# Three accumulators instead of four, eight gathers and then eight scatters a round, and a reordered first round in a one-core graph layer

## The chip, the cores and the metric

The kernel runs on one core of one Trainium2 chip. The metric is the device time of one execution in microseconds (us); lower is better. Three runs of the kernel before are at hand, and one further execution was profiled.

## The reference, cut to what matters

The program is one layer of a graph network over 6250 nodes with 256 features and 100000 edges, followed by a recurrent network over the nodes. The part that the change touches is the sum over the edges:

```python
xn = layernorm(x)
neigh = segment_sum(xn[src], dst, num_segments=n)   # 100000 rows gathered, summed by target
h = (1 + eps) * xn + neigh
h = relu(h @ W1 + b1) @ W2 + b2                      # then a batch norm over the nodes
x = x + h + attention_mix(xn)                        # linear attention: keys, values, queries
x = x + lstm_stage(layernorm(x))                     # 6250 sequential steps
```

## The kernel before, in words

The program is a row of blocks, and each block begins when all engines have ended the one before.

**Opening** (lines 174 to 266). `x` is loaded and normalised, and `xn_d`, the normalised rows in device memory, is stored. Between these stores SP issues the zeros for the accumulators `acc_d`, ten pieces of 640 KB for each of NA = 4 accumulators: 8 pieces first, 2 after each of ten pairs of stores, and the 12 that are left at the end (line 194).

**First edge block** (helpers from line 328, engine programs from line 513 to 708). The edges are taken in groups of 512, four columns of 128. A round is two groups, g = 0 and g = 1, and there are H2 = 50 rounds in this block. For each group:

- SP loads the source and target indices into `staged_i` (line 339), when the gathers of the same g a round earlier have landed and both its targets have been cast.
- POOL gathers four times 128 rows of `xn_d` into `rows` (line 348). `gather_group(h, g)` first waits for the sum of the group (h-1, g), since that sum reads the same half of `rows`.
- PE transposes the targets (line 378), and DVE compares them, which gives the 0/1 matrix `equal` (line 426), finds the rows that must go to a spare row because an earlier edge of the group has the same target (lines 429 to 434), and writes `target` (line 439). That last write waits until the scatters of (h-1, g) have landed, since they read the same half of `target`.
- PE multiplies `equal` with `rows` (line 389), which adds up edges with the same target; ACT copies the product to `sums` (line 400), also only after the scatters of (h-1, g) have landed. `sum_equal` waits for the copy of the group before, since there is one set of banks.
- POOL scatters the four columns with an accumulating indirect DMA (line 367). Column j goes to accumulator j, and a scatter waits until the last one into its accumulator has landed.

POOL's order in a round i of the first block is: gathers of (i, 1), scatters of (i, 0), gathers of (i+1, 0), scatters of (i, 1). In the same round the other engines also make keys and values for 125 nodes. On DVE (lines 671 to 703) the order is: casts; `find_equal(i, 0)`; keys and values, centred; `find_equal(i, 1)` with its `target` write; the variance, the root and `kvn` (lines 689 to 698); then `kvsum`. On PE (lines 583 to 604) it is: targets of (i, 0); the product for keys and values; targets of (i, 1); `sum_equal(i, 0)`; the product of `kvn` (line 597), which waits for DVE's `kvn`; `sum_equal(i, 1)`; the transposes of the next node rows. So `sum_equal(i, 1)` stands behind `kvn` of the same round, and `kvn` behind the `target` write of (i, 1). ACT (lines 627 to 639) squares, copies sums (i, 0), takes the root, copies sums (i, 1), and copies the next node rows. In rounds 1 to 9 some weights for the later stage are turned and split as well.

**Second edge block** (lines 741 to 866). Rounds 50 to 97, with the same groups; beside two rounds runs one chunk of 250 nodes of the attention: four products on PE. No key or value work stands between the two sums of a round.

**The stage after the edges** (lines 893 to 1060). For each of 25 chunks, SP loads the chunk's rows of all accumulators into `ht` (line 918), DVE adds them in two steps (lines 928 and 930) into `hsum`, PE transposes `hsum` (line 988), and two layers of products follow. **The rest** is a normalisation and the recurrent network, which no line of the change touches.

Of the kernel before, what the change touches and what calls it, by code (L numbers as in the profile page):

```python
# [27 lines left out]
ALU = mybir.AluOpType  # L28
# [13 lines left out]
GT = 4  # L42
# [5 lines left out]
NA = 4  # L48
# [10 lines left out]
ZS = 10  # L59
# [35 lines left out]
def gps_layer_kernel(nc, x, src, dst, gnn_eps, gW1, gb1, gW2, gb2, gamma, beta, w_qkv, b_qkv,  # L95
# [14 lines left out]
    with top, stage, nc.allow_non_contiguous_dma(reason="vectors of 256 numbers, loaded once"):  # L110
# [157 lines left out]
        with ExitStack() as st:  # L268
# [41 lines left out]
            scattered = [[sem(f"scattered{a}_{g}") for g in range(2)] for a in range(NA)]  # L310
# [42 lines left out]
            def scatter_group(pool, h, g, of=FULL):  # L353
# [4 lines left out]
                for j in range(T):  # L358
                    a = j
                    if not due(h) and not g:  # L360
                        pool.wait_ge(zero_out[a], 16 * (ZS + (a == NA - 1)))
                    if g:
                        pool.wait_ge(scattered[a][0], 16 * (h + 1))
                    elif due(16 * h):
                        pool.wait_ge(scattered[a][1], 16 * h)
# [4 lines left out]
                    ).then_inc(scattered[a][g], 16)  # L370
# [22 lines left out]
            def copy_sums(act, h, g, of=FULL):  # L393
                P, T = of
                act.wait_ge(summed, 2 * h + g + 1)
                for a in range(NA):
                    if due(16 * h):
                        act.wait_ge(scattered[a][g], 16 * h)
# [13 lines left out]
            def find_equal(dve, h, g, of=FULL):  # L412
# [23 lines left out]
                for a in range(NA):  # L436
                    if due(16 * h):
                        dve.wait_ge(scattered[a][g], 16 * h)
# [117 lines left out]
            def _(pool):  # L556
# [18 lines left out]
            def _(pe):  # L575
                kv_to = bank[3][0:R, :].rearrange("p (s h c) -> p s h c", s=2, h=HEADS)

                def body(i):
                    turn_targets(pe, i, 0)
                    if not due(i):  # L580
                        pe.wait_ge(mixw_in, 16 * MIX_LOADS)
# [9 lines left out]
                    sum_equal(pe, i, 0)  # L591
# [14 lines left out]
                turn_rows(pe, 0)  # L606
# [3 lines left out]
            def _(act):  # L610
# [16 lines left out]
                def body(i):  # L627
                    act.wait_ge(cen_ready, i + 1)
                    nc.scalar.activation(sq[:], cen[:], ACT.Square).then_inc(sq_ready, 1)
                    copy_sums(act, i, 0)  # L630
# [10 lines left out]
                copy_rows(act, 0)  # L641
# [3 lines left out]
            def _(dve):  # L645
# [7 lines left out]
                add_rows(dve, 0)  # L653

                def body(i):
# [18 lines left out]
                    if not due(i):  # L674
                        dve.wait_ge(mixw_in, 16 * MIX_LOADS)
# [1055 lines left out]
```

## Time and profile before

| | us |
|---|---|
| three runs | 16084.22, 16095.17, 16082.19; median 16084.22 |
| profiled execution, its own time | 16096.5 |
| its span | 16094.8 |
| PE busy | 12549.7 (78%) |
| DVE busy | 10109.2 (63%) |
| ACT busy | 5158.2 (32%) |
| POOL busy | 2040.0 (13%), all of it before 2664 |
| both edge blocks with the gaps between | 120 to 2671 |

POOL is GpSimd, DVE VectorE, ACT ScalarE, PE TensorE, SP SyncE. The shares over the whole span say little here: the recurrent network takes 13064 us of the 16095 and hides the stages before it. The edge blocks have to be read by themselves, in their own windows and in the timeline of a round.

### The profile page before, as it was taken

The page shows a single profiled execution, that of the slowest core. Times are in us where ns is not written, and L with a number is a line of the kernel's source. Part 1 is how long each engine was busy: PE and PEld are TensorE (multiplying, and loading weights), DVE is VectorE, ACT ScalarE, POOL GpSimd, SP SyncE. Part 2 cuts the span into 40 slices and gives each one's busy share as a digit, 9 for nine tenths or more (in the row PEclk, how much of TensorE's full clock was granted, in tenths as well). Part 3 has the DMA queues.
Part 4 walks back from the last instruction along what each step waited for, and adds up shares of the span by engine and source line. Part 5 has one row for each costly group of instructions (what it writes and reads, how often), then busy time and mean ns, then how long its engine had stood idle before and what let it go on. Part 6 is the DMA issues. An engine that isn't in the chain of part 4 may idle for free. (4 is left out here: it accounts for less than half of the span.)

```text
span 16094.8 us, 920575 instructions
## 1 busy us (share of the span) xinstructions
PE 12549.7 (78%) x375284; PEld 11596.3 (72%) x375284; DVE 10109.2 (63%) x84155; ACT 5158.2 (32%) x32368; POOL 2040.0 (13%) x1573
## 2 busy tenths in 40 slices
PE   3444446888888888888888888888888888888887
PEld 2333334788888888888888888888888888888886
DVE  4443222666666666666666666666666666666667
ACT  1111111333333333333333333333333333333333
POOL 5887885000000000000000000000000000000000
PEclk8666777555555555555555555555555555555556
DMA  6555554100000000000000000000000000000000
GB/s 169 90 91 84 83 83 99 67 2 2 2 2 2 2 2 2 2 2 2 2 2 2 2 2 2 2 2 2 2 2 2 2 2 2 2 2 2 2 2 17
DMA packets 622798, 340.12 MB, mean 21 GB/s; under 512 B 455829, under 2 KB 571433, under 8 KB 622134
## 3 DMA queue, kind: packets, MB, share of 16 engines
q0 software_dynamic: 150048, 204.90, 7.9%
q1 hardware_dynamic: 461968, 129.69, 3.9%
q10 hardware_dynamic: 10742, 5.06, 0.1%
q8 instruction: 19, 0.31, 0.0%
q14 instruction: 21, 0.16, 0.0%
HBM read 172.29 MB, written 160.65 MB: 21 GB/s over the span
## 5 line engine op out<-in xcount | busy, mean ns | idle before, releaser
L1363 PE MATMUL bank<-hrest,whh 128*128 128x1 bf16 (+1 forms) x300000 | 9080.9, 166 | 1920.2 <-DVE hrest L1487 1920.2
L1363 PEld LDWEIGHTS bank<-hrest,whh 128*128 128x128 bf16 x300000 | 8555.7, 104 | 2483.1 <-DVE hrest L1487 2482.7
L1431 ACT ACTIVATE gates<-bank 128x4 f32<-128x4 f32 x12500 | 2198.1, 176 | 8137.1 <-DVE bank L1468 7260.1
L1468 DVE TENSOR_REDUCE bank<-bank 128x4 f32<-128x12 f32 x12500 | 2212.9, 177 | 3178.9 <-PE bank L1363 2296.2
L1363 PE MATMUL bank<-xsteps,wih 128*128 128x15 bf16 (+1 forms) x60048 | 2715.4, 174 | 0.0
L1476 DVE CUSTOM_DVE_ANT_1 uv<-gates 128x4 f32<-128x4 f32 x12500 | 2041.6, 163 | 445.9
L1363 PEld LDWEIGHTS bank<-xsteps,wih 128*128 128x128 bf16 x60048 | 2278.7, 103 | 0.0
L1439 ACT ACTIVATE bank<-gates 128x1 f32<-128x1 f32 x12500 | 2188.1, 175 | 119.3
L1492 DVE TENSOR_TENSOR hrest<-hrest 128x1 f32<-128x1 f32 x12500 | 1993.3, 159 | 216.2
L1497 DVE TENSOR_TENSOR hrest<-hrest 128x1 f32<-128x1 f32 x12500 | 1981.5, 159 | 217.3
L1363 PE MATMUL bank<-ones,gbias 128*128 128x5 bf16 x10008 | 1679.9, 168 | 9.7 <-DMA xsteps<-x_d 9.7
L367 POOL DMA_INDIRECT acc_d<-sums,target x782 | 1263.5, 1616 | 255.9 <-issue 237.2
L389 PE MATMUL bank<-rows,equal 128*128 128x256 f32 x1564 | 688.4, 617 | 771.9 <-DMA rows<-xn_d,staged_i 729.9
L1435 ACT ACTIVATE og<-zo 128x1 f32<-128x1 f32 x6250 | 1171.4, 187 | 0.0
L389 PEld LDWEIGHTS bank<-rows,equal 128*128 128x128 f32 x1564 | 479.1, 321 | 918.7 <-issue 815.4
L1363 PEld LDWEIGHTS bank<-ones,gbias 128*128 128x128 bf16 x10008 | 1039.6, 104 | 10.1 <-issue 10.1
L1476 DVE DVE_READ_ACCUMULATOR2_ANT gates<- 128x1 f32 x12500 | 1040.1, 83 | 0.0
L1472 DVE TENSOR_REDUCE zo<-bank 128x1 f32<-128x3 f32 x6250 | 980.2, 157 | 0.0
L1487 DVE SCALAR_TENSOR_TENSOR hrest<-gates,bank 128x1 f32<-128x1 f32 x6250 | 970.8, 155 | 11.7
L1487 DVE SCALAR_TENSOR_TENSOR hrest<-og,bank 128x1 f32<-128x1 f32 x6250 | 972.1, 156 | 0.0
L348 POOL DMA_INDIRECT rows<-xn_d,staged_i x782 | 775.3, 991 | 248.2 <-issue 225.0
L400 ACT ACTIVATE sums<-bank 128x512 f32<-128x512 f32 x391 | 212.3, 595 | 1507.0 <-PE bank L389 1500.8
(167 smaller groups left out, 3295.4 us busy)
## 6 DMA issues: line engine op xcount, KB each, us to landing
acc_d<-zero SPq DMA_DIRECT2D x40, 640.0 KB, 12.6
ht<-acc_d SPq DMA_DIRECT2D x100, 224.0 KB
xsteps<-x_d SPq DMA_DIRECT2D x1252, 15.0 KB, 1.7
U<-hrest SPq DMA_DIRECT2D x1250, 5.0 KB, 1.7
x_d<-x SPq DMA_DIRECT2D x25, 750.0 KB, 3.2
rows<-xn_d,staged_i POOLq DMA_INDIRECT x782
acc_d<-sums,target POOLq DMA_INDIRECT x782, 3.8
xi<-xn_d SPq DMA_DIRECT2D x50, 125.0 KB
```

The lines of the kernel that those rows point to most:

```text
L367: pool.indirect_dma_start(out=acc_d[a], out_offset=bass.IndirectOffsetOnAxis(ap=target[0:P, g, j:j + 1], axis=0), in_=sums[0:P, g, j, :], ...
L389: last = nc.tensor.matmul(prod[j // 2][0:P, j % 2, :], equal[0:P, g, j, 0:P], rows[0:P, g, j, :], start=True, stop=True)
L1363: return nc.tensor.matmul(to, w, v, start=start, stop=True, skip_group_check=True)
L1431: nc.scalar.activation(gates[:, k, 0:2 * NG_[k]:2], zi[k], ACT.Tanh).then_inc(ifg_act[k], 1)
L1435: nc.scalar.activation(og[1], zo[:], ACT.Tanh).then_inc(o_act, 1)
L1439: nc.scalar.activation(tc[k], gates[:, k, 5:6], ACT.Tanh).then_inc(tc_ready[k], 1)
L1468: nc.vector.tensor_reduce(zi[k], gi[k][b][:, s], axis=AX.X, op=ALU.add).then_inc(ifg_summed[k], 1)
L1472: nc.vector.tensor_reduce(zo[:], go[b][:, s], axis=AX.X, op=ALU.add).then_inc(o_summed, 1)
L1476: nc.vector.tensor_tensor_reduce(out=uv[:, k, :].rearrange("p (a c) -> p a c", a=2), in0=gates[:, k, 0:4].rearrange("p (a c) -> p a c", a= ...
L1487: stt(out=hrest[:, 0, at, k:k + 1], in0=og[k], scalar=1.0, in1=tc[k], op0=ALU.add, op1=ALU.mult).then_inc(h1_ready[k], 1)
L1492: nc.vector.tensor_tensor(hrest[:, 1, at, k:k + 1], hrest[:, 0, at, k:k + 1], hpart[:, 0, at, k:k + 1], ALU.subtract).then_inc(h2_ready[k], 1)
L1497: nc.vector.tensor_tensor(hrest[:, 2, at, k:k + 1], hrest[:, 1, at, k:k + 1], hpart[:, 1, at, k:k + 1], ALU.subtract).then_inc(h3_ready[k], 1)
```

## The change

It does five things. The number of accumulators falls from four to three, with their zeros and loads. A round's eight scatters go to accumulators 0, 1, 2, 0, 1, 2, 0, 1, each waiting for the one three places before it, or, for the first three, for the last one of the round before into the same accumulator. POOL's order becomes both gather groups of round i+1, then both scatter groups of round i. In round 0 the targets, the sum and the copy of group (0, 0) go ahead of the node rows, keys and values. The sum over accumulators in the later stage becomes two additions of one accumulator each.

```diff
-NA = 4
+NA = 3
 def scatter_group(pool, h, g, of=FULL):
                 for j in range(T):
-                    a = j
-                    if not due(h) and not g:
-                        pool.wait_ge(zero_out[a], 16 * (ZS + (a == NA - 1)))
-                    if g:
-                        pool.wait_ge(scattered[a][0], 16 * (h + 1))
-                    elif due(16 * h):
-                        pool.wait_ge(scattered[a][1], 16 * h)
+                    place = GT * g + j
+                    a = place % NA
+                    if place >= NA:
+                        before = place - NA
+                        pool.wait_ge(scattered[before % GT][before // GT], 16 * (h + 1))
+                    else:
+                        if not due(h):
+                            pool.wait_ge(zero_out[a], 16 * (ZS + (a == NA - 1)))
+                        before = 2 * GT - 1
+                        while before % NA != a:
+                            before -= 1
+                        if due(16 * h):
+                            pool.wait_ge(scattered[before % GT][before // GT], 16 * h)
...
 # POOL, first edge block
                 gather_group(pool, 0, 0, first=True)
+                gather_group(pool, 0, 1, first=True)
                 def body(i):
-                    gather_group(pool, i, 1)
+                    gather_group(pool, i + 1, 0)
+                    gather_group(pool, i + 1, 1)
                     scatter_group(pool, i, 0)
-                    gather_group(pool, i + 1, 0)
                     scatter_group(pool, i, 1)
                 first_apart(pool, H2 - 1, body)
-                gather_group(pool, H2 - 1, 1)
                 scatter_group(pool, H2 - 1, 0)
                 scatter_group(pool, H2 - 1, 1)
...
 # PE, first edge block
                     turn_targets(pe, i, 0)
                     if not due(i):
+                        sum_equal(pe, i, 0)
+                        turn_rows(pe, i)
                         pe.wait_ge(mixw_in, 16 * MIX_LOADS)
...
                     turn_targets(pe, i, 1)
-                    sum_equal(pe, i, 0)
+                    if due(i):
+                        sum_equal(pe, i, 0)
...
 # POOL, second edge block
                 gather_group(pool, H2, 0)
-                with pool.Fori(H2, HL, 1) as h:
-                    gather_group(pool, h, 1)
+                gather_group(pool, H2, 1)
+                with pool.Fori(H2, HL - 1, 1) as h:
+                    gather_group(pool, h + 1, 0)
+                    gather_group(pool, h + 1, 1)
                     scatter_group(pool, h, 0)
-                    gather_group(pool, h + 1, 0)
                     scatter_group(pool, h, 1)
+                gather_group(pool, HL, 0)
                 gather_group(pool, HL, 1, of=LAST)
+                scatter_group(pool, HL - 1, 0)
+                scatter_group(pool, HL - 1, 1)
...
 # DVE, the stage after the edges
-                    nc.vector.tensor_tensor(ht[:, b, 0:2], ht[:, b, 0:2], ht[:, b, 2:4], ALU.add).then_inc(pair_ready, 1)
+                    nc.vector.tensor_tensor(ht[:, b, 0], ht[:, b, 0], ht[:, b, 1], ALU.add).then_inc(pair_ready, 1)
                     dve.wait_ge(pair_ready, c + 1)
-                    nc.vector.tensor_tensor(hsum[:, b], ht[:, b, 0], ht[:, b, 1], ALU.add).then_inc(hsum_ready, 1)
+                    nc.vector.tensor_tensor(hsum[:, b], ht[:, b, 0], ht[:, b, 2], ALU.add).then_inc(hsum_ready, 1)
```

On ACT and DVE of the first block round 0 is reordered in the same way (`copy_sums(0, 0)` and `copy_rows(0)` first; `add_rows(0)` behind `find_equal(0, 0)`). No line of DVE, PE or ACT changes for the rounds from 1 on, apart from the names of the semaphores that they wait for.

## Rows read from the trace of the kernel before

**Rows 1.** Page, section 2: the span in 40 slices, busy tenths of each.

```profile
POOL 5887885000000000000000000000000000000000
PEclk8666777555555555555555555555555555555556
```

**Rows 2.** Windows by stage: length, then busy time and (count) per engine, PEclk, DMA share, GB/s.

```profile
165.56:1417.32 1251.76, 556.99 (x1760) 392.96 (x1760) 611.93 (x1385) 188.00 (x449) 1017.41 (x768) 0.68 0.55 91
...
1461.00:2650.06 1189.06, 581.12 (x1785) 448.04 (x1784) 283.48 (x633) 142.48 (x283) 961.31 (x748) 0.71 0.52 83
...
2671.45:2897.00 225.55, 187.65 (x900) 160.55 (x900) 88.78 (x137) 63.77 (x152) 0.00 (x0) 0.96 0.39 118
...
3030.00:16094.00 13064.00, 11069.89 (x370356) 10483.85 (x370356) 8957.28 (x81487) 4704.76 (x31352) 0.00 (x0) 0.50 0.02 2
```

**Rows 3.** Groups on POOL, window 165.56:1417.32: busy us, mean ns, idle before and releasers.

```profile
L367 POOL DMA_INDIRECT acc_d<-sums,target x384 | 634.3, 1652 | 117.3 <-issue 116.7 <-ACT sums L400 0.6
L348 POOL DMA_INDIRECT rows<-xn_d,staged_i x384 | 383.2, 998 | 117.0 <-issue 103.9 <-ACT sums L400 10.1 <-DMA acc_d<-sums,target 2.7
```

**Rows 4.** The same for the window 1461:2650.06.

```profile
L367 POOL DMA_INDIRECT acc_d<-sums,target x376 | 594.5, 1581 | 117.1 <-issue 113.7 <-ACT sums L400 2.7 <-PE bank L389 0.3
L348 POOL DMA_INDIRECT rows<-xn_d,staged_i x372 | 366.8, 986 | 113.4 <-issue 113.4
```

**Rows 5.** Timeline of one round: start, us, engine, line, operation, idle time before it.

```profile
999.99 1.02 POOL L348 DMA_INDIRECT rows<-xn_d,staged_i  x1 [0.30 <-issue]
...
1002.05 0.16 DVE L439 TENSOR_TENSOR target<-dstf,move 128x4 int32<-128x4 f32 x1 [7.29 <-DMA acc_d<-sums,target]
...
1002.61 0.94 POOL L348 DMA_INDIRECT rows<-xn_d,staged_i  x1 [0.30 <-issue]
...
1005.11 2.13 POOL L367 DMA_INDIRECT acc_d<-sums,target  x1 [0.30 <-issue]
...
1006.50 0.69 DVE L698 TENSOR_TENSOR kvn<-kvn,kv_b 125x512 f32<-125x512 f32 x1
...
1007.25 1.22 PE L597 MATMUL bank<-kvn 125*128 125x128 f32 x4 [9.72 <-DVE kvn L698]
...
1008.26 3.13 PE L389 MATMUL bank<-rows,equal 128*128 128x256 f32 x8
...
1011.30 1.55 POOL L367 DMA_INDIRECT acc_d<-sums,target  x1 [0.30 <-issue]
...
1018.71 1.62 POOL L367 DMA_INDIRECT acc_d<-sums,target  x1 [0.30 <-issue]
```

**Rows 6.** Timeline, the last rounds of the first edge block.

```profile
1415.75 1.57 POOL L367 DMA_INDIRECT acc_d<-sums,target  x1 [0.31 <-issue]
...
1425.57 3.62 PE L389 MATMUL bank<-rows,equal 128*128 128x256 f32 x8
...
1429.23 1.08 ACT L400 ACTIVATE sums<-bank 128x512 f32<-128x512 f32 x2 [8.06 <-PE bank L389]
1431.19 1.55 POOL L367 DMA_INDIRECT acc_d<-sums,target  x1 [1.03 <-issue]
```

**Rows 7.** Tile acc_d, window 165.56:1417.32.

```profile
DMA to landing us min/median/max: 3.6/3.8/4.4
```

**Rows 8.** Timeline of the opening: the last zero stores, and the start of the first edge block.

```profile
99.01 19.24 SPq L194 DMA_DIRECT2D acc_d<-zero  x14
...
136.17 0.38 ACT L527 ACTIVATE xk<-bank 128x250 f32<-128x250 f32 x1 [87.59 <-PE bank L519]
...
151.32 3.23 PE L389 MATMUL bank<-rows,equal 128*128 128x256 f32 x8
...
163.99 1.57 POOL L367 DMA_INDIRECT acc_d<-sums,target  x1 [0.31 <-issue]
```

**Rows 9.** Waits of PE in the stage after the edges: us, times, longest.

```profile
PE bank L988 <- DVE hsum L930: 15.6, 20, 1.8
```

**Rows 10.** Groups on DVE in the same stage.

```profile
L928 DVE TENSOR_TENSOR ht<-ht 125x1024 f32<-125x1024 f32 x25 | 30.6, 1224 | 26.1 <-DMA ht<-acc_d 25.4
```

More of the change, by code:

```diff
@@ L309, in gps_layer_kernel @@
             gathered = [sem(f"gathered{g}") for g in range(2)]
-            scattered = [[sem(f"scattered{a}_{g}") for g in range(2)] for a in range(NA)]
+            scattered = [[sem(f"scattered{j}_{g}") for g in range(2)] for j in range(GT)]
             cast, dst_turned = sem("cast"), sem("dst_turned")
@@ L369, in scatter_group @@
                         in_=sums[0:P, g, j, :], in_offset=None, compute_op=ALU.add,
-                    ).then_inc(scattered[a][g], 16)
+                    ).then_inc(scattered[j][g], 16)
             def turn_targets(pe, h, g, of=FULL):
@@ L395, in copy_sums @@
                 act.wait_ge(summed, 2 * h + g + 1)
-                for a in range(NA):
+                for j in range(GT):
                     if due(16 * h):
-                        act.wait_ge(scattered[a][g], 16 * h)
+                        act.wait_ge(scattered[j][g], 16 * h)
                 for m in range(T // 2):
@@ L435, in find_equal @@
                                                     in1=dup[0:P, 0:T], op0=ALU.subtract, op1=ALU.mult))
-                for a in range(NA):
+                for j in range(GT):
                     if due(16 * h):
-                        dve.wait_ge(scattered[a][g], 16 * h)
+                        dve.wait_ge(scattered[j][g], 16 * h)
                 nc.vector.tensor_tensor(target[0:P, g, 0:T], dstf[0:P, g, 0:T], move[0:P, 0:T], ALU.subtract)\
@@ L627, in body @@
                 def body(i):
+                    if not due(i):
+                        copy_sums(act, i, 0)
+                        copy_rows(act, i)
                     act.wait_ge(cen_ready, i + 1)
                     nc.scalar.activation(sq[:], cen[:], ACT.Square).then_inc(sq_ready, 1)
-                    copy_sums(act, i, 0)
+                    if due(i):
+                        copy_sums(act, i, 0)
                     act.wait_ge(gvar_ready, i + 1)
@@ L652, in _ @@
                 links = 5 + REFINE_STEPS
-                add_rows(dve, 0)
                 def body(i):
@@ L674, in body @@
                     if not due(i):
+                        add_rows(dve, i)
                         dve.wait_ge(mixw_in, 16 * MIX_LOADS)
@@ L752, in _ @@
                 gather_group(pool, H2, 0)
-                with pool.Fori(H2, HL, 1) as h:
-                    gather_group(pool, h, 1)
+                gather_group(pool, H2, 1)
+                with pool.Fori(H2, HL - 1, 1) as h:
+                    gather_group(pool, h + 1, 0)
+                    gather_group(pool, h + 1, 1)
                     scatter_group(pool, h, 0)
-                    gather_group(pool, h + 1, 0)
                     scatter_group(pool, h, 1)
+                gather_group(pool, HL, 0)
                 gather_group(pool, HL, 1, of=LAST)
+                scatter_group(pool, HL - 1, 0)
+                scatter_group(pool, HL - 1, 1)
                 scatter_group(pool, HL, 0)
                 scatter_group(pool, HL, 1, LAST)
-                for a in range(NA):
-                    pool.wait_ge(scattered[a][0], 16 * (HL + 1))
-                    pool.wait_ge(scattered[a][1], 16 * (HL + (a < LAST[1])))
+                for j in range(GT):
+                    pool.wait_ge(scattered[j][0], 16 * (HL + 1))
+                    pool.wait_ge(scattered[j][1], 16 * (HL + (j < LAST[1])))
             @block.tensor
```

2 lines of the change are left out of this document (removed).

## The prediction

> **What bounds the kernel now.** Times of the trace are in us. I read the slices of the page first [rows 1]: POOL works only at the start, and what the change touches lies there. The windows by stage [rows 2] then put a length on it: 1251.8 for 48 rounds of the first edge block, 1189.1 for most of the second, 225.6 for the stage after the edges, 13064 for the recurrent network, which the change leaves alone. In both edge blocks POOL is the busiest engine (81%); DVE has 49% and 24%, and the DMA engines are busy 0.55 and 0.52.
>
> Whether POOL is really the limit shows in its groups [rows 3, 4]: 384 gathers of 0.998 and 384 scatters of 1.652 in the first block, 0.986 and 1.581 in the second, and before each of them an idle time of 0.305 put down to "issue", nothing else to speak of. Eight of each with their gaps are 8 x (1.303 + 1.957) = 26.1 a round, and the window gives 1251.76 / 48 = 26.08. So POOL never stands still in the first block; a round costs what its sixteen DMA instructions cost. The same for the second: 8 x (1.291 + 1.886) = 25.4.
>
> The change neither adds nor removes one of these sixteen. It can gain only in what lies around them, and lose wherever POOL begins to wait. So the next view is the timeline of a round [rows 5], to see how much room each of POOL's waits has.
>
> **The wait that the new order meets.** Call the end of the last scatter of (i-1, 1) the mark. In the round shown it is at 999.69 (999.99 less the gap of 0.30). Behind it a chain runs over four engines: the scatter lands, DVE's `target` write of (i, 1), which waited 7.29 for that landing, begins at 1002.05; the variance, root and `kvn` end at 1007.19; PE's product of `kvn` begins at 1007.25, and `sum_equal(i, 1)` runs from 1008.26 to 1011.39. That is 11.7 after the mark. At the end of the block [rows 6] the mark is 1417.32 and the same sum ends at 1429.19: 11.9. Over all rounds of the window I take 12.0.
>
> Who needs this sum? The gathers of (i+1, 1), which overwrite the half of `rows` that it reads. Before the change they come a whole round after the mark, 26 against 12, and POOL meets the wait long satisfied. After it POOL's order behind the mark is gathers (i+1, 0), then gathers (i+1, 1): only four gathers, 4 x 1.303 = 5.2, lie between. The chain itself is not shortened, because no line of DVE or PE changes for rounds from 1 on: `sum_equal(i, 1)` still stands behind `kvn`, and `kvn` behind the landing of scatters that are now directly ahead of the gathers. So POOL must stop there in every round, and behind the stopped gathers are queued the eight scatters that start the next chain. The cycle closes on itself.
>
> Its length: 12.0 to the end of the sum; then POOL's waking. A gather's waking from a stop is not shown for this semaphore; the nearest row is a scatter that waited for ACT's copy: the copy ended at 1430.31, the scatter began at 1431.19 [rows 6], so 0.9. The bounds are 0.1 (the releases between the other engines in rows 5) and 1.0. Then four gathers with three gaps, 4 x 0.998 + 3 x 0.305 = 4.9, and eight scatters with eight gaps, 8 x 1.957 = 15.7. Together 33.5.
>
> Two small things come off. A first gather behind scatters takes 1.02 against 0.94 for a later one, a first scatter 1.62 against 1.55 [rows 5]; with the second of each run that is some 0.1 for each change of kind, and there are half as many: 0.1 off the scatters. And the scatters average 1.652 here against 1.581 in the second block; the excess, 8 x 0.071 = 0.57 a round, sits in single scatters such as the one at 1005.11, which took 2.13 while DVE made `kvn` [rows 3, 4, 5]. In the new order `kvn` falls into POOL's gathers and its stop, but other DVE work falls on the scatters. I take half off, 0.3. The Trainium skill ("SBUF — State Buffer", section "Who interferes with whom") has a rule for this: a VectorE instruction with two SBUF inputs contends with a GpSimd instruction that reads SBUF. By it the `kvn` multiplication and addition would no longer lengthen scatters, and the whole 0.57 could go, 13 us more off the sum than my half; the trace agrees as far as the one long scatter shows.
>
> A round of the first block becomes 33.5 - 0.1 - 0.3 = 33.0 (rounded down), 6.9 more than 26.1, and from the last scatter of round 0 to that of round 48 there are 48 such rounds: **+331**.
>
> I looked for a second stop in this block. Scatters (i, 0) now land 7.6 before those of (i, 1), and DVE needs about 5 from the `target` write of (i, 0) to the next one; the gathers of (i+1, 0) need `sum_equal(i, 0)`, which stands ahead of `kvn`; the indices are loaded a round earlier than before. Each has more than 2 to spare.
>
> **The opening.** Ten of forty pieces of zeros go. The last fourteen took SP 19.24 to issue [rows 8], 1.37 each, so the block could begin 13.7 earlier; the last stores of `xn_d`, issued just before these fourteen, must land first, and I take 12. Round 0: ACT's own DMA issues stand before its first copy at 136.17, so reordering round 0 moves the keys and values no further forward than those 12. `sum_equal(0, 1)` ended at 154.55 [rows 8], now 142.5; but the gathers of (1, 1) wait for it and the scatters of round 0 for them: 142.5 + 0.9 + 4.9 + 15.7 = 164.0 for the end of the last scatter of round 0, against 165.56 before. **-2.** The 12 gained are nearly all eaten by the new order at once; bounds -12 and +5.
>
> **The end of the first block.** The last copy waits for the same chain and `sum_equal(49, 1)` before and after: nothing, within 2.
>
> **The second block.** No `kvn` stands between the sums. `sum_equal(h, 1)` needs the copy of (h, 0), which needs the landing of scatters (h-1, 0). From their end: 2.3 to the landing (3.8 from a scatter's start, less its 1.57 [rows 7, 6]), 1.1 for a copy, 3.1 to 3.6 for the sum and about 2 for an attention product between, 0.9 to wake: 10. Between them and the gathers of (h+1, 1) lie four scatters and four gathers, 12.7. The wait is covered with 2 or 3 to spare; if that cover is gone, each us costs 47. What is left is one change of kind fewer per round, 2 x 0.1: **-9**. Its start and its end I put at **-2** together (the start has a sum to wait for before the second gathers; at the end gathers come earlier), within 5.
>
> **Three accumulators.** A scatter now waits for the third before it. That one lands 3.6 to 4.4 after its start [rows 7] and the scatter starts 3 x 1.86 = 5.6 after it; with 0.9 to wake, 5.3 at most. Nothing, by 0.3.
>
> **The stage after the edges.** PE waited 15.6 over 20 chunks for `hsum` [rows 9]. The first addition, 1.224 on 1024 elements [rows 10], becomes one of half the size, some 0.69, and a quarter less is loaded. That takes 0.53 x 20 = 11 off, up to 15.6: **-13**. The recurrent network: nothing.
>
> **The sum.** 331 - 2 - 9 - 2 - 13 = **+305**. Against the profiled execution's own 16096.5 (its span is 16094.8) that is 16401.5; this execution stands 12.3 above the median of the three runs, 16084.2, so for a median I forecast 16084.2 + 305, about **16390**, 1.9% slower.
>
> **Rivals.**
> 1. *The chain is faster than I take it.* PE's part, 1.0 to the sum and 3.1 to 3.6 for it, is at a granted clock of half (1.2 GHz) much of the time; the windows' mean is 0.68 [rows 2]. At 2.4 GHz about 2 of the 12 would go, and with a wake of 0.1 a little more: some 100 to 130 off, about 16280. For it speaks that the mean is not 0.5; against it that PE will be idle longer in each round, with the same work.
> 2. *No stop: faster.* If `sum_equal(i, 1)` ended within 5.2 of the mark, POOL would stay the limit and only the gains would be left: 12 from the opening, 0.2 x 97 = 19 from fewer changes of kind, 13 from the later stage, 44 in all: 16040. The deciding point is the place of the gathers of (i+1, 1), 5.2 behind the mark; the rows show 11.7 and 11.9, and landing plus DVE alone are 7.5. For it speaks only that DVE or PE might have slack that I read as need.
> 3. *Scatters queue behind one another.* If in a run of eight the landing came at 4.9 or later instead of 3.8, each wait on three accumulators would bite; at 0.9 more per three scatters, 0.3 x 760 = 228 on top: 16620. Against it: the DMA engines are busy 0.55, and no landing of the window is over 4.4.
> 4. *The cover in the second block is thinner than 2*: 47 per us, inside the range above the forecast.
>
> **Chances.** Forecast with the upper part of rival 4: 0.74. Rival 1: 0.13. Rival 2: 0.06, with 0.02 for a change within the bound. Rival 3: 0.05. A measurement of this kernel can tell about 0.2%, 32 us, from no change; so faster 0.06, same 0.02, slower 0.92. Bounds of a round's excess are 5.2 (most of rival 1 with a short waking) and 7.6 (nothing taken off): 250 to 365, less 26 and 10 either way: 16290 to 16450.
>
> **What would show it.** In the first edge block POOL idle about 7 to 8 in each round in front of the gathers of (i+1, 1), released by PE's sum (or ACT's copy after it), a period near 33, and POOL's share down from 81% to about 64%; the second block with POOL's gaps at 0.305 throughout and a period near 25.2; `hsum` waits gone on PE. A first block with rounds near 26 makes the forecast wrong and rival 2 right; gaps in front of single scatters inside a run speak for rival 3.

## The result, and the profile after

Four runs of each kernel on one chip: 16373.65 after the change (median; 16369.55 to 16377.94) against 16084.92 before (16082.19 to 16095.17). The ratio is **1.0179**, 95% interval 1.0166 to 1.0192: slower, 288.7 us by the medians. The forecast was 16390.

The profiled executions are 16096.5 before and 16369.55 after, 273.0 apart. The one of before lies above all four of its runs, that of after is the lowest of its four; that makes the rest of the 288.7. Cut at marks that both traces have, the 273.0 fall on these pieces:

| piece | before | after | difference | predicted |
|---|---|---|---|---|
| start to the end of round 0's last scatter | 165.56 | 160.85 | -4.7 | -2 |
| 48 rounds of the first edge block | 1251.76 | 1572.18 | +320.4 | +331 |
| from there to the last scatter of all | 1246.25 | 1238.04 | -8.2 | -11 |
| from there to the recurrent network's first load (3030.52 and 3314.29) | 366.95 | 343.22 | -23.7 | -13 |
| the rest | 13064.3 | 13053.5 | -10.8 | 0 |
| sum | | | +273.0 | +305 |

The windows by stage of the kernel after (length, busy time and count per engine, PEclk, DMA share, GB/s): first block, second block with the boundary before it, the stage after the edges (all 25 chunks), the recurrent network.

```profile
160.85:1733.03 1572.18, 492.47 (x1760) 360.23 (x1760) 607.26 (x1385) 182.97 (x448) 983.63 (x769) 0.64 0.44 73
1733.03:2971.07 1238.04, 582.15 (x1854) 447.62 (x1855) 288.04 (x666) 147.67 (x295) 985.42 (x772) 0.67 0.52 82
2978.90:3195.60 216.70, 193.76 (x938) 170.10 (x938) 82.03 (x158) 70.81 (x167) 0.00 (x0) 0.93 0.32 94
3314.29:16367.80 13053.51, 11066.50 (x370356) 10480.01 (x370356) 8937.23 (x81487) 4680.37 (x31352) 0.00 (x0) 0.50 0.02 2
```

In the first line POOL has the same 768 instructions as in [rows 2] (and one at the window's edge), and even 34 less busy time, in a window 320 longer: its share fell from 81% to 63%. The page's slices say the same at a glance. Where [rows 1] had 8, 8 and 7 in the second to fourth slice, there is now 6, 6 and 6, and POOL works one slice longer:

```profile
POOL 4666788200000000000000000000000000000000
PEclk7666666755555555555555555555555555555556
```

POOL's groups in the first edge block, window 160.85:1733.03 (busy us, mean ns, idle before and releasers):

```profile
L373 POOL DMA_INDIRECT acc_d<-sums,target x385 | 611.6, 1589 | 118.1 <-issue 110.9 <-DMA acc_d<-sums,target 7.2
L348 POOL DMA_INDIRECT rows<-xn_d,staged_i x384 | 373.7, 973 | 470.7 <-issue 470.7
```

Its waits in the same window (us in total, times, longest):

```profile
POOL rows L348 <- issue: 470.7, 384, 7.9
POOL acc_d L373 <- issue: 110.9, 362, 0.5
POOL acc_d L373 <- DMA acc_d<-sums,target: 7.2, 23, 0.5
```

Against [rows 3] one number has changed much: the idle time ahead of the gathers, 117.0 to 470.7. That is 354 more, over 48 rounds 7.4 a round; the longest single stop is 7.9. The instructions themselves have become a little shorter: a scatter fell from 1.652 to 1.589, a gather from 0.998 to 0.973, 0.7 a round together. What is left is 320.4 / 48 = 6.67 more a round, a period of 32.75.

Where the stop stands in a round shows in the timeline (start, us, engine, line, operation, idle time before it):

```profile
1011.07 1.74 POOL L373 DMA_INDIRECT acc_d<-sums,target  x1 [0.30 <-issue]
...
1015.22 0.16 DVE L445 TENSOR_TENSOR target<-dstf,move 128x4 int32<-128x4 f32 x1 [2.86 <-DMA acc_d<-sums,target]
...
1016.97 0.95 POOL L348 DMA_INDIRECT rows<-xn_d,staged_i  x1 [0.30 <-issue]
...
1019.62 0.69 DVE L709 TENSOR_TENSOR kvn<-kvn,kv_b 125x512 f32<-125x512 f32 x1
...
1020.36 1.23 PE L606 MATMUL bank<-kvn 125*128 125x128 f32 x4 [22.61 <-DVE kvn L709]
...
1021.38 3.35 PE L395 MATMUL bank<-rows,equal 128*128 128x256 f32 x8
...
1025.53 0.94 POOL L348 DMA_INDIRECT rows<-xn_d,staged_i  x1 [7.61 <-issue]
...
1030.68 1.63 POOL L373 DMA_INDIRECT acc_d<-sums,target  x1 [0.30 <-issue]
```

The last scatter of the round before ends at 1012.81: that is the mark. From it the landing and `target` take 2.4, `kvn` is ready at 7.5, the sum begins at 8.6 and ends at 11.9, and the gather that needs its half of `rows` starts 0.80 later. POOL had ended the four gathers before it at 1017.92 and stood for 7.61. PE's product waited 22.61 for `kvn`: no other work of PE lies between. The landing is as before in the median [rows 7]; the longest is 4.8 where it was 4.4. `acc_d` in this window:

```profile
DMA to landing us min/median/max: 3.6/3.8/4.8
```

In the second edge block the period is 25.27 against 25.42 and POOL's gaps stay at 0.31 in the mean (window 1775:2936.34; the periods of this block are taken over the 44 rounds that end with its 46th):

```profile
L373 POOL DMA_INDIRECT acc_d<-sums,target x368 | 577.1, 1568 | 112.8 <-issue 105.5 <-DMA acc_d<-sums,target 7.3
L348 POOL DMA_INDIRECT rows<-xn_d,staged_i x368 | 360.1, 979 | 112.6 <-issue 101.0 <-DVE target L445 5.8 <-ACT sums L406 5.8
```

Beside [rows 4], the scatters went from 1.581 to 1.568. The opening's timeline shows the ten pieces of zeros gone (4 issued at the end instead of the 14 of [rows 8]) and two stops of POOL in their place, one for the indices of group (1, 0) and one for the sum of (0, 1):

```profile
100.91 5.33 SPq L194 DMA_DIRECT2D acc_d<-zero  x4
...
129.55 0.95 POOL L348 DMA_INDIRECT rows<-xn_d,staged_i  x1 [10.65 <-DMA staged_i<-in_dst]
...
140.56 0.95 POOL L348 DMA_INDIRECT rows<-xn_d,staged_i  x1 [6.11 <-issue]
```

In the stage after the edges PE no longer waits for `hsum` at all ([rows 9]: 15.6), and the whole stage took 216.70 against 240.00 before (2671.45 to 2911.45; the window of [rows 2] stops at 2897, before the last chunks are done).

### The profile page after: what moved, and what is told of

Its sections match the earlier page's. It is cut to its first block and busy times, and to the rows that moved or that the text cites. A ratio compares the mean times of both kernels' runs of the same rounds, so it can differ in the third digit from the quotient of the medians.

```text
span 16367.8 us, 920271 instructions
## 1 busy us (share of the span) xinstructions
PE 12450.8 (76%) x375284; PEld 11540.8 (71%) x375284; DVE 10061.5 (61%) x84155; ACT 5128.3 (31%) x32368; POOL 1999.1 (12%) x1573
## 5 line engine op out<-in xcount | busy, mean ns | idle before, releaser
L395 PE MATMUL bank<-rows,equal 128*128 128x256 f32 x1564 | 544.8, 510 | 437.0 <-ACT sums L406 426.3
L606 PE MATMUL bank<-kvn 125*128 125x128 f32 x200 | 61.1, 461 | 1054.9 <-DVE kvn L709 1054.9
```

## The experiments

The theory (A): POOL's new order closes a cycle over landing, `kvn`, PE's sum and the gathers, and costs the 330; the three accumulators cost nothing and gain a little. The main rival (B): the three accumulators or the longer waits of scatters are what costs. Kernels are called by the number of their experiment, so kernel 2 is that of experiment 2. Gaps and periods below are read from each kernel's timeline as in the table above. Where a kernel was timed several times (kernels 1, 2, 8 and 10), its median and its ratio to the kernel before stand, with a 95% interval; the others have a single time, given beside the median of the kernel before on the same chip.

### 1. The order undone, three accumulators kept

```diff
                 def body(i):
-                    gather_group(pool, i + 1, 0)
-                    gather_group(pool, i + 1, 1)
+                    gather_group(pool, i, 1)
                     scatter_group(pool, i, 0)
+                    gather_group(pool, i + 1, 0)
                     scatter_group(pool, i, 1)
```

(with `gather_group(pool, H2 - 1, 1)` behind the loop again; first block only)

> The changed kernel with one part undone: in the first edge block POOL takes gathers (i, 1), scatters (i, 0), gathers (i+1, 0), scatters (i, 1) again; three accumulators, the new first round, the new order of the second block and the additions stay. Theory A (the gathers of (i+1, 1) stand too close behind the scatters of (i-1, 1), and the sum they wait for ends 12 us after them): the stop of 7.1 us a round goes, a round of the first block is 26.1 us, and the kernel takes about 16373.7 less 320 = 16050 us. Rival B (three accumulators make the scatters wait): the loss stays, 16370 us, with idle time in front of scatters.

Measured: 16047.15, ratio 0.9973 (0.9963 to 0.9984). Period 26.11, round 0 ends at 149.11. POOL's groups of the first block, window 149.11:1402.53:

```profile
L373 POOL DMA_INDIRECT acc_d<-sums,target x384 | 635.0, 1654 | 119.0 <-issue 106.6 <-PE bank L395 6.7 <-DMA acc_d<-sums,target 3.7
L348 POOL DMA_INDIRECT rows<-xn_d,staged_i x384 | 382.4, 996 | 117.0 <-issue 103.3 <-ACT sums L406 10.1 <-DMA acc_d<-sums,target 3.3
```

The idle time ahead of the gathers, 470.7 in the kernel after, is 117.0 again, with three accumulators. B falls. One edit of POOL's order is worth 1.0179 against 0.9973, about 330 us: 48 x (32.75 - 26.11) = 319 in the rounds and 160.85 - 149.11 = 12 in round 0.

### 2. The new order kept, PE's sum ahead of `kvn`

```diff
+                    sum_equal(pe, i, 1)
                     pe.wait_ge(kvn_ready, i + 1)
...
                     last.then_inc(kv_prod, 1)
-                    sum_equal(pe, i, 1)
```

> The changed kernel with POOL's order kept and the chain cut instead: on PE sum_equal(i, 1) stands directly behind sum_equal(i, 0), ahead of the product of kvn. Theory A: the sum then needs only the targets' comparison and ACT's copy of (i, 0), both done before the last scatter of the round before, so POOL has no stop; a round of the first block is 25.3 us, as in the second block, and the kernel takes 16373.7 less 48 x 7.4 = 355, about 16020 us, less than both kernels. Rival B: nothing changes, 16370 us. Rival C (POOL stops for the landing of eight scatters in a row, whatever PE does): rounds stay near 32 us.

Measured: 16047.61, ratio 0.9974 (0.9963 to 0.9984). The stops are gone from all rounds of the block but the first, which shows that the cycle closed through PE's program order and not through the data. But the period is 26.11, not 25.3. POOL's groups, window 159.09:1412.47:

```profile
L373 POOL DMA_INDIRECT acc_d<-sums,target x384 | 615.4, 1603 | 119.9 <-issue 109.4 <-DMA acc_d<-sums,target 10.5
L348 POOL DMA_INDIRECT rows<-xn_d,staged_i x384 | 401.0, 1044 | 117.0 <-issue 103.6 <-ACT sums L406 13.4
```

No gap has grown; but beside kernel 1 the gathers have grown, from 0.996 to 1.044, while the scatters fell only from 1.654 to 1.603. The reason shows in a round of this kernel's timeline:

```profile
1002.74 0.69 DVE L707 TENSOR_TENSOR kvn<-cen,grstd 125x512 f32<-125x512 f32 x1
1002.80 1.45 POOL L348 DMA_INDIRECT rows<-xn_d,staged_i  x1 [0.30 <-ACT sums L406]
...
1004.19 0.69 DVE L709 TENSOR_TENSOR kvn<-kvn,kv_b 125x512 f32<-125x512 f32 x1
1004.55 1.14 POOL L348 DMA_INDIRECT rows<-xn_d,staged_i  x1 [0.30 <-issue]
...
1006.00 0.95 POOL L348 DMA_INDIRECT rows<-xn_d,staged_i  x1 [0.30 <-issue]
...
1019.69 0.69 DVE L695 TENSOR_TENSOR cen<-kv,gsum 125x512 f32<-125x512 f32 x1
1019.75 2.06 POOL L373 DMA_INDIRECT acc_d<-sums,target  x1 [0.30 <-issue]
```

A gather that starts 0.06 into a DVE multiplication with both inputs in SBUF takes 1.45, one with none beside it 0.95; the scatter that starts 0.06 into `cen` takes 2.06 instead of 1.55. How far into the instruction it starts matters: the gather that starts 0.36 into `kvn`'s addition takes only 1.14. The new order moves the `kvn` instructions from the scatters onto the gathers and takes little off. And in round 0 POOL stood 13.75 for the indices of (1, 0), since this kernel too gathers round 1 before it scatters round 0:

```profile
133.22 0.98 POOL L348 DMA_INDIRECT rows<-xn_d,staged_i  x1 [13.75 <-DMA staged_i<-in_dst]
```

So eight and eight without the stop is worth no more than the old order.

### 3. The new order with four accumulators

```diff
-NA = 3
+NA = 4
```

(with the two additions of the kernel before)

> The changed kernel with four accumulators again (zeros, scatters to accumulators 0 to 3 twice, four loads and the addition of 1024 elements in the later stage), POOL's new orders kept. Theory A: the first block keeps its rounds of 32.75 us and its stops of 7.1 us; only the opening (12 us later), and the stage after the edges (23 us longer) go back, about 16405 us. Rival B: the stops go and the kernel is near 16090 us.

Measured: 16424.12 (before 16091.63). Period 32.71, and 48 stops of 6.82 to 7.88, mean 7.62. POOL's gathers in the window 178.67:1748.92, and the stage after the edges with PE's waits in it:

```profile
L348 POOL DMA_INDIRECT rows<-xn_d,staged_i x384 | 375.1, 977 | 468.3 <-issue 468.3
```

```profile
2993.90:3234.99 241.09, 199.23 (x938) 169.10 (x938) 96.46 (x158) 70.69 (x167) 0.00 (x0) 0.93 0.37 111
```

```profile
PE bank L1003 <- DVE hsum L945: 16.7, 21, 1.8
```

The stop is the same with four accumulators. Against the kernel after, 17.8 are lost by the end of round 0 (178.67 against 160.85) and 24.4 in the stage after the edges (241.09 against 216.70). Both are larger than the prediction had taken (12 for the zeros, 13 for the stage). The next two take the 24 apart.

### 4. A fourth load in the stage after the edges

```diff
-                    for a in range(NA):
-                        rows_ = acc_d[a][...]
+                    for a in range(NA + 1):
+                        rows_ = acc_d[a % NA][...]
```

(the kernel after, with room for the fourth part and its wait; the additions leave the fourth part out)

> The changed kernel with a fourth, unused load in the stage after the edges (accumulator 0 once more, into a fourth part of ht, and waited for); the additions stay two of 512 elements. The stage took 240.0 us before and 216.7 us after. If the smaller addition gave the 23 us, the stage stays at 217 us. If the loads did (PE waited for sums that waited for loads), it goes back to 235 to 240 us. Everything ahead of the stage stays as it is.

Measured: 16391.07 (before 16091.63). The stage and PE's waits in it:

```profile
2984.55:3213.61 229.06, 198.05 (x938) 171.47 (x938) 83.13 (x158) 70.70 (x167) 0.00 (x0) 0.92 0.39 117
```

```profile
PE bank L1003 <- DVE hsum L945: 7.0, 9, 1.1
```

That is 12.4 over the 216.70, between the two expectations: the fourth load alone costs half of the difference.

### 5. The wide addition, with three loads

```diff
-nc.vector.tensor_tensor(ht[:, b, 0], ht[:, b, 0], ht[:, b, 1], ALU.add)
+nc.vector.tensor_tensor(wide[:, b], ht[:, b, 0:2], ht[:, b, 1:3], ALU.add)
```

(on kernel 1, `hsum` then from `wide[:, b, 0]` and `ht[:, b, 2]`: two columns of 512 added, as before the change)

> x1_order_undone with a first addition of 1024 elements in the stage after the edges (half of it unused, into a tile of its own), three loads as they are. x4_fourth_load gave 229.1 us for the stage against 216.7 in the changed kernel and 240.0 before: a quarter more loading costs 12. If the rest is the addition, the stage is here 216.7 + 11 to 13, about 229 us; if PE has slack for 0.5 us a chunk once the loads are early, it stays at 217 to 219 us, and loads and addition cost only together.

Measured: 16053.96 (before 16087.83). The stage in kernel 1, then in this one with PE's waits:

```profile
2650.44:2867.75 217.31, 193.71 (x938) 170.14 (x938) 82.12 (x158) 70.70 (x167) 0.00 (x0) 0.93 0.32 94
```

```profile
2659.95:2886.45 226.50, 199.73 (x938) 170.16 (x938) 95.82 (x158) 70.68 (x167) 0.00 (x0) 0.92 0.30 90
```

```profile
PE bank L1004 <- DVE hsum L946: 3.7, 15, 0.4
```

That is 9.2 more. With the 12.4 of the load it makes 21.6 of the 23.3 by which the stage fell.

### 6. Two accumulators

```diff
-NA = 3
+NA = 2
```

(on kernel 2, with one addition in the later stage)

> x2_sum_ahead with two accumulators (two loads and one addition in the later stage). A scatter then waits for the second before it, which starts 3.7 us earlier and lands 3.8 us after its start. If POOL's waking of 0.8 to 0.9 us comes on top of every such wait, a scatter inside a run starts 4.7 us after the second before it: 0.5 us more for each of six scatters of a run, 2.9 us a round, 98 rounds, 285 us; less some 30 to 35 for fewer zeros, loads and additions: about 16300 us. If only the landing counts (POOL's sequencer waits ahead of the engine), it costs 0.1 us a wait at most: 16020 to 16070 us, and three accumulators have 1.8 us of room instead of 0.9.

Measured: 16331.15 (before 16087.83). Periods 29.21 and 28.22, against 26.11 and 25.23 in kernel 2: 3.1 and 3.0 more a round. POOL's scatters, window 150.16:1552.23, and three in a row from the second block's timeline:

```profile
L373 POOL DMA_INDIRECT acc_d<-sums,target x384 | 623.4, 1624 | 261.9 <-DMA acc_d<-sums,target 155.3 <-issue 106.5
```

```profile
2000.93 1.55 POOL L373 DMA_INDIRECT acc_d<-sums,target  x1 [1.17 <-DMA acc_d<-sums,target]
2002.85 1.56 POOL L373 DMA_INDIRECT acc_d<-sums,target  x1 [0.37 <-issue]
2005.46 1.55 POOL L373 DMA_INDIRECT acc_d<-sums,target  x1 [1.05 <-DMA acc_d<-sums,target]
```

Two scatters start 1.92 and 2.61 apart in turn, 4.53 from one to the next into the same accumulator. That is about the landing, 3.8 after the start in the median, and 0.79 for POOL to wake: where this trace shows a scatter waiting for a landing, it starts 0.79 after it nearly every time. With three accumulators the starts are 5.6 apart: about 1 to spare. The stage after the edges stays at 216.7, so going from three accumulators to two brings nothing there; with three, PE already never waited for `hsum`.

### 7. Kernel 2 without two of `kvn`'s instructions

```diff
-step(nc.vector.tensor_tensor(kvn[:], cen[:], spread(grstd[:]), ALU.mult))
-step(nc.vector.tensor_tensor(kvn_s, kvn_s, gain_of(kv_g), ALU.mult))
-nc.vector.tensor_tensor(kvn_s, kvn_s, gain_of(kv_b), ALU.add).then_inc(kvn_ready, 1)
+nc.vector.tensor_tensor(kvn[:], cen[:], spread(grstd[:]), ALU.mult).then_inc(kvn_ready, 1)
```

This leaves out gain and bias of the normalised keys and values.

> x2_sum_ahead without the gain and the bias of the normalised keys and values (DVE's multiplication and addition, 0.69 us each with both inputs in SBUF, left out; one chain link fewer for each). In x2_sum_ahead a round of the first block takes 26.1 us although POOL has no stop, against 25.2 in the second block: gathers average 1.044 us against 0.974. Theory A: DVE instructions with both inputs in SBUF lengthen POOL's indirect DMAs that run beside them; without these two, gathers go back to about 0.98 and a round to about 25.6 us, 20 to 25 us less in all. Rival: the longer gathers have to do with the traffic of the scatters that land at that time, or with the order of gathers and scatters; then the round stays at 26.1 us.

Measured: 16043.81 (before 16087.83). Period 25.78, 0.33 less. The gathers average 1.015 instead of 1.044. In the timeline one long gather is left, beside the one instruction that is left:

```profile
1016.02 0.69 DVE L707 TENSOR_TENSOR kvn<-cen,grstd 125x512 f32<-125x512 f32 x1
1016.09 1.44 POOL L348 DMA_INDIRECT rows<-xn_d,staged_i  x1 [0.30 <-ACT sums L406]
1017.83 0.95 POOL L348 DMA_INDIRECT rows<-xn_d,staged_i  x1 [0.30 <-issue]
```

In kernel 2 the gather after the long one took 1.14; here it takes 0.95. The direction is as expected, the size is not (0.33 against 0.5). The trace of kernel 2 shows why: in nearly every round one gather starts 0.06 into `kvn`'s first multiplication (0.48 a round), and one 0.36 into its addition (0.20 a round). Leaving out the last two instructions takes away only the second. Of 48 x 0.33 = 16, 5.9 are left at the last scatter of all, since this kernel's second block ran at 25.46 a round, 0.23 above kernel 2's, with no edit there.

### 8. Kernel 2 with round 0's first scatters ahead

```diff
                 def body(i):
+                    if not due(i):
+                        scatter_group(pool, i, 0)
                     gather_group(pool, i + 1, 0)
                     gather_group(pool, i + 1, 1)
-                    scatter_group(pool, i, 0)
+                    if due(i):
+                        scatter_group(pool, i, 0)
                     scatter_group(pool, i, 1)
```

> The changed kernel with sum_equal(i, 1) ahead of the product of kvn (as in x2_sum_ahead), and in round 0 alone POOL scatters (0, 0) before it gathers round 1. In x2_sum_ahead POOL stood 13.8 us in the opening in front of the gathers of (1, 0), for their indices, with the sums of (0, 0) ready; in x1_order_undone the first scatter started at 123.4 and round 0 ended at 149.1, against 159.1. If that idle time is worth filling, round 0 ends about 10 us earlier than in x2_sum_ahead and the whole is near 16037 us; if POOL is held by sum (0, 1) or its copy anyway, nothing changes, 16047 us.

Measured: 16042.35, ratio 0.9972 (0.9962 to 0.9983). Round 0 ends at 150.32 instead of 159.09, 8.8 earlier: POOL scatters in the time in which it stood for indices. At the last scatter of all 2.1 of that is left (2642.33 against 2644.45); the second block's period was 25.34 against 25.23, again with no edit there. The totals of kernels 2 and 8 are not told apart.

### 9. The old first round

Kernel 1 with `turn_rows(0)`, `copy_rows(0)` and `add_rows(0)` ahead of the loops, and the sum and the copy of (0, 0) where they were before.

> x1_order_undone with the first round of the kernel before on PE, ACT and DVE as well (node rows, keys and values of round 0 ahead of its targets and sums). In x1_order_undone the first scatter started at 123.4 us (128.9 in x7_wide_add, whose opening is the same) and the last of round 0 ended at 149.1 (155.3). If the reordered first round is worth something, the first scatter waits here for ACT's copy behind the centred keys and values, about 12 us earlier than the 145.5 of the kernel before: near 133, and round 0 ends at 153 to 156. The rival is that the second group's copy sets the end of round 0 in any case, so that it ends at 149 to 152.

Measured: 16043.86 (before 16106.83 on that chip). The first scatter starts at 132.2, against 123.4 in kernel 1 and 128.9 in kernel 5, which has the same opening as kernel 1. Round 0 ends at 152.81, against 149.11 and 155.28. Two kernels with the same opening differ by 6 at the end of round 0, and the old first round lies between them there, though its first scatter is the latest of the three by 3: what the reordering of round 0 is worth could not be told.

### 10. Kernel 8 with `earlier` made from PSUM

```diff
+for j in range(T):
+    made = nc.vector.scalar_tensor_tensor(out=earlier[0:P, j, 0:P], in0=turned[0:P, j, 0:P],
+                                          scalar=dstf[0:P, g, j:j + 1], in1=below[0:P, 0:P],
+                                          op0=ALU.is_equal, op1=ALU.mult)
 nc.vector.tensor_tensor(equal[0:P, g, 0:T, 0:P], turned[0:P, 0:T, 0:P], mine, ALU.is_equal)
-step(nc.vector.tensor_tensor(earlier[...], equal[...], below[...], ALU.mult))
```

`turned` is a PSUM bank, so the 512-element instruction with two inputs from SBUF is replaced by four of 128 with one.

> x6_first_scatters with DVE's product for earlier duplicates (equal by below, 128x512, both inputs in SBUF) replaced by four instructions that compare the targets in PSUM with the column's own target and multiply by below in one step (one tensor input in SBUF). If instructions with two SBUF inputs lengthen POOL's indirect DMAs, the long gathers and scatters beside them go in both blocks: a round of the first block falls from 26.13 to about 25.9 us and of the second from 25.34 to 25.2, 10 to 20 us in all, near 16027 us. If not, the time stays at 16042 us; if the comparison that now comes about 1 us later delays a sum on which POOL waits, it rises.

Measured: 16045.71 against 16106.83 on that chip, ratio **0.9962** (0.9948 to 0.9975), the lowest of all; kernel 8 has 0.9972, and the intervals overlap. Periods 25.90 and 25.12, against 26.14 and 25.34 in kernel 8; the last scatter of all ends at 2623.86, 18.5 earlier than in kernel 8. The total doesn't show it: in the profiled execution the recurrent network, which no edit touches, took 25.4 more than in kernel 8's. The groups of the first block, 150.74:1394.18:

```profile
L373 POOL DMA_INDIRECT acc_d<-sums,target x385 | 610.5, 1586 | 120.6 <-issue 106.3 <-DMA acc_d<-sums,target 13.7 <-PE bank L395 0.3
L348 POOL DMA_INDIRECT rows<-xn_d,staged_i x384 | 397.2, 1034 | 117.0 <-issue 107.6 <-ACT sums L406 9.4
```

And two scatters of a round, beside the DVE instructions that start near them:

```profile
1004.26 1.55 POOL L373 DMA_INDIRECT acc_d<-sums,target  x1 [0.30 <-DMA acc_d<-sums,target]
1004.32 0.69 DVE L700 TENSOR_TENSOR cen<-kv,gsum 125x512 f32<-125x512 f32 x1
...
1006.08 0.69 DVE L437 TENSOR_TENSOR equal<-bank,dstf 128x512 f32<-128x512 f32 x1
1006.12 1.57 POOL L373 DMA_INDIRECT acc_d<-sums,target  x1 [0.30 <-issue]
```

A scatter that starts 0.04 into a DVE instruction with one input in PSUM takes 1.57, as if nothing were beside it. One that started 0.06 ahead of `cen` was not lengthened either, where kernel 2's, 0.06 behind its start, took 2.06. So a kernel's time also depends on the phase, that is, on how often a start happens to fall into such an instruction.

How much is phase can be counted in the traces. The table takes the same 44 rounds of the second block in six kernels whose code for these rounds is the same, but for kernel 10's edit. It has the gathers and scatters that start while `earlier` is being made, and what they take over the ordinary 0.95 and 1.55 (0.07 more for the first of a run):

| kernel | starts inside `earlier` | extra, a round | period | period less extra |
|---|---|---|---|---|
| after | 32 | 0.15 | 25.27 | 25.12 |
| 1 | 28 | 0.19 | 25.29 | 25.11 |
| 2 | 28 | 0.12 | 25.23 | 25.11 |
| 7 | 44 | 0.34 | 25.46 | 25.12 |
| 8 | 34 | 0.23 | 25.34 | 25.11 |
| 10 | 37, and none lengthened | 0.00 | 25.12 | 25.12 |

This one instruction accounts for the differences between the second blocks. The kernels with the old instruction differ by phase; kernel 10's 0.22 a round against kernel 8 is the instruction that went. In the first block it is less clear: of the 0.24 that kernel 10 gained there, 0.09 stood beside `earlier` in kernel 8, and most of the rest beside `cen` and `kvn`, which are unchanged: phase.

## Why the prediction was right

**The stop.** Its place (ahead of the gathers of (i+1, 1)), its size and its cause came as written: stops of 7.1 to 7.9, mean 7.7, where 7 to 8 stood, a period of 32.75 where 33.0 stood, POOL at 63% where 64% stood. (The range of 16290 to 16450 is rounded outward: the sums given for it make 16298 and 16433.) The chain's terms, as means over the 48 rounds: the sum ended 11.99 behind the mark (taken 12.0), POOL woke 0.80 after it, in every one of them (taken 0.9, between bounds of 0.1 and 1.0), four gathers took 4.80 (taken 4.9), and eight scatters with their gaps 15.16 (taken 15.7, less the 0.4 that comes off). Together they are the 32.75. That the cause is the place of PE's sum behind `kvn` is shown by kernel 2. Kernel 1 shows that without POOL's new order in the first block the rest of the change costs nothing. Rival 1, a faster chain, did not come: the granted clock of the block fell from 0.68 to 0.64 instead of rising, and the sum took 3.46 in the mean where it had taken 3.40. One reading was announced wrongly: the profile puts the stop down to "issue" and not to PE's sum. The releaser had to be found by the time at which the sum ended.

**The 11 too many in the 48 rounds** (331 against 320.4) are 0.1 a round of waking, 0.1 of the four gathers behind the stop, and contention on the scatters, less 0.1 that the prediction had rounded away. For the scatters I took 0.1 off for fewer changes of kind and 0.3, half of the 0.57. They fell by 8 x 0.063 = 0.5, so 0.4 of it is contention. `kvn` now falls into the stop, where POOL issues nothing: in the kernel before, the starts inside its first multiplication cost 0.44 a round, and in the kernel after there are none. What is left stands beside `earlier`. (The other four gathers became shorter too, but they lie beside the chain and count for nothing.) The Trainium skill ("SBUF — State Buffer", section "Who interferes with whom") says that a VectorE instruction with two SBUF inputs contends with a GpSimd instruction that reads SBUF. The trace agrees for `kvn`; of the 0.57 that the prediction gave as possible by this rule 0.4 went, since `earlier`, with two SBUF inputs as well, still stands beside POOL's instructions. The timelines of kernels 2, 7 and 10 show it instruction by instruction: 1.45 or 1.44 against 0.95, 2.06 against 1.55, and 1.57 beside an instruction with one input in PSUM.

**The opening**: -4.7 against -2, inside its bounds. I had seen only the stop for the sum. The one of 10.65 for the indices of (1, 0) was missed; it didn't decide, since the sum of (0, 1) stood last all the same. That sum let the gathers start at 140.56, so it ended near 139.8 where I had 142.5. How much of this is the reordered round 0 isn't known (kernel 9).

**The second block and the boundary**: -8.2 against -11. The period fell by 0.15 where 0.2 stood. The gaps ahead of the gathers stay at 0.31, so the wait on the sum was covered, and by more than the 2 to 3 of the prediction: from the block's second round on the sum ended 5.5 or more before the start of the first gather that needs it, of which POOL's waking would take 0.8.

**Three accumulators cost nothing**: right. 23 waits in the first block, the longest 0.5. Kernel 6 shows the same arithmetic (landing and waking against the distance of the scatters) biting when the distance is two: 3.1 and 3.0 a round where 2.9 was expected from it.

**The stage after the edges**: -13 against -23.7, the term that was mis-sized. The 11 for the narrower addition was near (9.2, kernel 5). What I held to be only the rest of PE's waits, the quarter less loaded, is worth another 12.4 (kernel 4). The step that failed is "up to 15.6": I took the waits of PE's transposes for `hsum` as all that could be gained. The weight loads of the same transposes have a row of their own, and in the same window of the kernel before they wait longer:

```profile
PEld bank L988 <- DVE hsum L930: 24.1, 22, 2.2
```

Over the whole stage these waits are 25.1 before and none after, for 23.3 gained; in kernel 3 they are 25.5 for 24.4, in kernel 4 11.3 for 12.4, in kernel 5 12.7 for 9.2. So this row would have been the better bound; that it is the cause no run separates.

**The recurrent network** took 10.8 less without a changed line. That is within the spread between executions: over all the kernels here, none of which changes it, it took from 13047.0 (kernel 5) to 13076.6 (kernel 1). It is a part of why the sum of 305 fits the difference of the medians, 288.7, better than that of the two profiles, 273.0.

**A step that failed in an expectation**: for kernel 2 I expected 25.3 a round. It took for granted that scatters without `kvn` beside them cost what they cost in the second block, and forgot that the gathers would then have `kvn` beside them. The first block was thereby expected 0.8 x 48 = 38 too short. What kernel 2 has gained over the kernel before, 44, lies in the opening (6.5), the second block (47 x 0.19 = 9) and the stage after the edges (some 23). Rival 2 of the prediction also had 44 for a kernel without the stop, but by luck: it counted 12, 19 (half of it in the first block, where nothing was gained) and 13.

**Open**: what round 0's new order is worth; what sets the phase in which DVE and POOL meet, which kernels with the same code for a block do not share; and why the stage after the edges gained more than the waits of PE's transposes.

## What to carry to other kernels

When an engine's order is changed so that a buffer is written again sooner, follow who reads it last, on every engine's program order and not only by data: a sum that stands behind work it doesn't need turned a wait with 14 us of room into a stop of 7.7 in every round of the first block. Cost a batch by the cycle it closes (landing, chain, waking, the batch itself), and count buffers by landing plus waking against their distance in time. And a part that saves (one accumulator fewer, some 40 us here) can be had without the part that costs: try each half of a change by itself.

## What was not expected of the hardware

- A gather or scatter on POOL that starts 0.06 into a DVE instruction of 0.69 with both inputs in SBUF takes about 0.5 more (0.95 to 1.45, 1.55 to 2.06). The later it starts, the less it costs: at 0.36 into `kvn`'s addition 0.19 (kernel 2), and the scatter at 1011.07 of the kernel after, 0.39 into `earlier` (1010.68, 0.69 long), took 1.74, 0.19 more. One that starts 0.06 ahead of such an instruction takes its normal time.
- Beside `equal`, which has one input in PSUM and is as long, none of 788 starts in all the traces here took more than 0.09 over the ordinary, and 0.07 of that is what the first of a run takes in any case.
- Three loads a chunk instead of four shortened a stage by 12.4, though the DMA engines were busy only 0.39 of the time with four (kernel 4) and 0.32 with three.
- POOL goes on 0.80 after the end of the PE sum that it stands for, in all 48 rounds, and 0.79 after a landing (kernel 6), beside a gap of 0.30 when it doesn't stand.
